# A fused cross-attention and FFN kernel: FFN tiles of 512 tokens in place of 256, raw weights rounded in place

## What is computed

```python
kv = (ctx @ W_src.T + b_src) * mask[:, :, None]        # keys 256, values 256
q  = (layernorm(x) @ W_tgt.T + b_tgt) * mask[:, :, None]
a  = softmax(where(mask == 0, -inf, q_h @ k_h.T / sqrt(32)))   # 8 heads of 32, per sequence
x  = x + concat(layernorm(x), a @ v) @ W_out.T + b_out
n  = layernorm(x)
h  = silu((n @ w1.T) * s1) * ((n @ w2.T) * s2)         # 256 -> 1024, weights in {-1, 0, 1}
h  = gelu((h @ h1.T) * s3)                             # 1024 -> 1024
h  = gelu((h @ h2.T) * s4)                             # 1024 -> 1024
out = x + (h @ w3.T) * s5                              # 1024 -> 256
```

## Time and profile before

| | |
|---|---|
| runs | median 1019.88 us of 3 (1019.52 to 1020.92) |
| profiled execution, first to last instruction | 1017.2 us (no other time of it is given) |
| busy | PE 968.1 us (95%), PEld 919.0, DVE 594.4 (58%), ACT 407.0 (40%), POOL 55.4 |
| chain that ended last, share of the span | PE 89%, DVE 6%, issue 3%, ACT 1%, DMA 1% |
| mean granted TensorE clock | 0.983 |
| HBM | 28.48 MB read, 4.19 MB written, 32 GB/s over the span |

### The profile page before, as it was taken

The page is one execution under the profiler, slowest core; times in us unless marked ns, Lnnn a source line. Parts: engine busy times, 40 slices in busy tenths (PEclk is TensorE's granted clock), DMA queues, the critical chain, the costliest instruction groups (busy, mean ns, idle before and its releaser), DMA issues.

```text
span 1017.2 us, 21299 instructions
## 1 busy us (share of the span) xinstructions
PE 968.1 (95%) x7936; PEld 919.0 (90%) x7936; DVE 594.4 (58%) x1232; ACT 407.0 (40%) x1110; POOL 55.4 (5%) x89
## 2 busy tenths in 40 slices
PE   5468999999999999999999999999999999999998
PEld 4268999999999999999999999999999999999998
DVE  5876464745747465574746657474574646556452
ACT  4735252352525325252432625234262523526231
POOL 1010000001000000100001010000100000010000
PEclk8779999999999999999999999999999999999999
DMA  8621010000001000000100001000000100000000
GB/s 315 220 83 38 9 41 1 21 26 21 26 0 46 0 21 26 21 26 0 41 5 21 26 10 36 0 21 26 21 26 0 46 0 21 26 10 0 0 11 11
DMA packets 18311, 32.99 MB, mean 32 GB/s; under 512 B 4336, under 2 KB 10864, under 8 KB 18288
## 3 DMA queue, kind: packets, MB, share of 16 engines
q1 hardware_dynamic: 18288, 32.68, 9.8%
HBM read 28.48 MB, written 4.19 MB: 32 GB/s over the span
## 4 chain that ended last, share of the span: by engine, by line
PE 89%; DVE 6%; issue 3%; ACT 1%; DMA 1%; SPq 1%; DVEq 0%; POOL 0%; ACTq 0%
PE F L413 57%; PE F L478 6%; PE G L386 6%; PE G L337 5%; PE G L320 5%; PE G L363 3%; PE G L329 3%; DVE pr L740 2%; PE G L374 2%; PE S L349 1%; DVE stage L915 1%; DVE g L794 1%; PE G L310 1%; DVE hAh L811 1%; PE G L396 1%
## 5 line engine op out<-in xcount | busy, mean ns | idle before, releaser
L413 PE MATMUL F<-hBh,H 128*128 128x256 f32 x1024 | 253.4, 289 | 0.7 <-DVE hBl L813 0.7
L413 PE MATMUL F<-hAh,H 128*128 128x256 f32 x1024 | 252.1, 288 | 0.5 <-DVE hAl L813 0.5
L413 PE MATMUL F<-hBl,H 128*128 128x256 f32 x1024 | 245.1, 282 | 0.0
L413 PE MATMUL F<-hAl,H 128*128 128x256 f32 x1024 | 244.9, 281 | 0.0
L574 ACT ACTIVATE g<-F,scols 128x256 f32<-128x256 f32 x256 | 107.4, 471 | 292.7 <-PE F L413 292.5
L413 PEld LDWEIGHTS F<-hAh,H 128*128 128x128 f32 x1024 | 193.0, 188 | 4.2 <-issue 2.8
L413 PEld LDWEIGHTS F<-hBh,H 128*128 128x128 f32 x1024 | 193.5, 189 | 1.7 <-DVE hBl L813 0.9
L413 PEld LDWEIGHTS F<-hAl,H 128*128 128x128 f32 x1024 | 193.7, 189 | 0.4
L413 PEld LDWEIGHTS F<-hBl,H 128*128 128x128 f32 x1024 | 193.3, 189 | 0.7
L413 PE MATMUL F<-x2h,W 128*128 128x256 f32 x512 | 132.6, 298 | 0.4
L811 DVE CAST hAh<-g 128x512 fp32r<-128x512 f32 x128 | 54.7, 427 | 120.6 <-ACT g L574 119.0
(11 more groups left out here) (80 smaller groups left out, 1253.1 us busy)
## 6 DMA issues: line engine op xcount, KB each, us to landing
cT<-ctx_t SPq DMA_DIRECT2D x16, 512.0 KB, 3.3
stage<-h SPq DMA_DIRECT2D x10, 512.0 KB, 5.6
x_in<-x_t SPq DMA_DIRECT2D x16, 256.0 KB, 2.6
out<-sil_y SPq DMA_DIRECT2D x32, 128.0 KB, 1.7
stage<-w SPq DMA_DIRECT2D x6, 512.0 KB, 7.0
mrow<-mask_row SPq DMA_DIRECT2D x16, 128.0 KB, 3.2
g<-h SPq DMA_DIRECT2D x3, 512.0 KB, 6.1
sil_y<-h SPq DMA_DIRECT2D x3, 512.0 KB, 6.2
```

What stands on the lines that cost most here:

```text
L413: ins = mm(bank, W[:, k, cols], part[:, k, :], start=first, stop=last)
```

## The change

**512 tokens.** `WIDE` = 512 and `TILES` = 8. The buffers `x2h`, `x2l`, `hAh` to `hBl`, `g`, `sil`, `x1` and `res` hold 512 tokens, F0 and F1 one block of 512 columns each. Each FFN matmul before W3 has 512 moving columns in place of 256, and there are half as many. W3's matmuls keep their 256 columns (its weights move, the tokens are stationary), and their number stays.

**Slots.** A tile is a list of 44 slots. Slots 0 to 7 are one gate and one up block each, 8 to 39 half a block each of the middle layers, 40 to 43 W3 for four groups of 128 tokens (`j`), of which the last two reuse F0 and F1. The attention works on halves of 256 tokens: half 0 in slots 0 to 21, half 1 in slots 22 to 43, at the same positions (`pos`) in each.

**Weights.** Every piece lands in the memory of its own weight buffer (`W1_raw` is the same bytes as `W1`), DVE looks at its low 16 bits first (a maximum over 1024 16-bit values), and ACT casts it in place. All 22 looks and casts stand in the prologue, which now holds both halves of the first 512 tokens, one look in each even slot and one cast in each odd one.

**Small ones.** `res` is written by ACT (`keep_residual`) and also takes the result; `pT` and `vb` are gone (the transposed probabilities go back into `pr`, `v` is scaled in place); WO is loaded ahead of the first piece; the flag is read once.

```diff
+HALVES = B // NB
+WIDE = 2 * T
+TILES = B * P // WIDE
+NJ = WIDE // P
...
+SLOTS = 44
+HALF = SLOTS // 2
...
-        stage = [sb(f"stage{i}", [P, CH]) for i in range(4)]
+        def with_raw(name, k, m):
+            at_byte = -(-nc.sbuf_base // 32) * 32
+            rounded = sb(name, [P, k, m], F32R)
+            return rounded, nc.alloc_sbuf_tensor_at(name + "_raw", [P, k, m], F32, offset=at_byte)
+        W1, W1_raw = with_raw("W1", KD, HID)
...
-        F = [st.enter_context(nc.psum_tensor(f"F{i}", [P, 2, T], F32)) for i in range(2)]
+        x2h, x2l = sb("x2h", [P, KD, WIDE], F32R), sb("x2l", [P, KD, WIDE], F32R)
+        hAh, hAl = sb("hAh", [P, KH, WIDE], F32R), sb("hAl", [P, KH, WIDE], F32R)
+        hBh, hBl = sb("hBh", [P, KH, WIDE], F32R), sb("hBl", [P, KH, WIDE], F32R)
+        g, sil = sb("g", [P, 2, WIDE]), sb("sil", [P, 2, WIDE])
+        F = [st.enter_context(nc.psum_tensor(f"F{i}", [P, WIDE], F32)) for i in range(2)]
...
-        landing = [s[:] for s in stage] + [g[:].rearrange("p q h t -> p (q h t)"), sil_y[:]]
...
+            def load_chunk(n):
+                src, _, raw, ks = chunks[n]
+                sp.dma_start(raw[:, ks, :], src[:, ks, :]).then_inc(chunk_loaded[n], 16)
...
+            sp.dma_start(WO[:], woT).then_inc(wo_loaded, 16)
+            sp.dma_start(scols[:], s_cols).then_inc(scales_loaded, 16)
+            sp.dma_start(s3_bc[:], s3.broadcast_to([P, D])).then_inc(scales_loaded, 16)
+            for n in range(2 * KD + KH):
+                load_chunk(n)
+            load_tile(1)
+            for n in range(2 * KD + KH, CHUNKS):
+                load_chunk(n)
+            load_tile(2)
...
+            def attention(a, pos):
+                if pos == 0:
+                    transposes_x(a)
+                if pos == 1:
+                    project_k(a)
+                    project_q(a)
...
+                if pos == 8:
+                    project_v(a, 0)
+                    project_v(a, 1)
...
+                if pos == 18:
+                    out_proj(a, 1)
+                if pos == 19:
+                    transpose_x2(a, 0)
+                if pos == 21:
+                    transpose_x2(a, 1)
...
+            def gate_up(f, m, general):
+                pe.wait_ge(x2_ready, at("x2_ready", 2 * f + 1, 2))
+                if m == 0:
+                    pe.wait_ge(scaled, at("scaled", f - 1, 3))
+                else:
+                    pe.wait_ge(sil_ready, at("sil_ready", f, m))
+                cols = slice(m * P, (m + 1) * P)
+                for k in range(KD):
+                    ins = group(F[0][:], W1, W1_raw, k, cols, x2h, x2l, KD - 1, general)
+                ins.then_inc(gate_done, 1)
+                if m == 0:
+                    pe.wait_ge(scaled, at("scaled", f - 1, 4))
+                else:
+                    pe.wait_ge(g_ready, at("g_ready", f, m))
+                for k in range(KD):
+                    ins = group(F[1][:], W2, W2_raw, k, cols, x2h, x2l, KD - 1, general)
+                ins.then_inc(up_done, 1)
...
+                if j >= 2:
+                    pe.wait_ge(scaled, at("scaled", f, j - 1))
...
+            def ffn(f, slot, general):
+                if slot < 8:
+                    gate_up(f, slot, general)
+                elif slot < 40:
+                    half = slot % 2
+                    middle(f, 8 + (slot - 8) // 2, range(4 * half, 4 * half + 4), general)
+                elif slot == 40:
+                    ffn_out(f, 0, range(7), general)
+                    ffn_out(f, 1, range(7), general)
+                elif slot == 41:
+                    ffn_out(f, 0, (7,), general)
+                    ffn_out(f, 1, (7,), general)
                 else:
...
+                    ffn_out(f, slot - 40, range(8), general)
+            def tile(f, s, general):
+                for slot in range(SLOTS):
+                    if s is not None:
+                        attention(2 * s + slot // HALF, slot % HALF)
+                    if f is not None:
+                        ffn(f, slot, general)
...
-            def silu(f, q):
-                act.wait_ge(gate_done, at("gate_done", f, q + 1))
-                for p in (2 * q, 2 * q + 1):
-                    act.wait_ge(g_ready, at("g_ready", f, max(p - 1, 0)))
-                    fn(sil[:, p % 2, :], F[0][:, p % 2, :], ACT.Silu, scale=scols[:, p:p + 1]).then_inc(sil_ready, 1)
+            def silu(f, m):
+                act.wait_ge(gate_done, at("gate_done", f, m + 1))
+                act.wait_ge(g_ready, at("g_ready", f, max(m - 1, 0)))
+                act.wait_ge(y_ready, at("y_ready", f - 1, 4))
+                fn(sil[:, m % 2, :], F[0][:], ACT.Silu, scale=scols[:, m:m + 1]).then_inc(sil_ready, 1)
...
+                if pos == 8:
                     exps(a, 0)
                     exps(a, 1)
+                    scale_v(a)
...
+            def keep_residual(f):
+                act.wait_ge(x1_ready, at("x1_ready", 2 * f + 1, 2))
+                act.wait_ge(stored, at("stored", f - 1, 64))
+                fn(res[:], x1[:], ACT.Copy).then_inc(res_ready, 1)
+            def ffn(f, slot):
+                if slot < 8:
+                    silu(f, slot)
+                    if slot == 2:
+                        keep_residual(f)
+                elif slot < 40 and slot % 2:
+                    gelu(f, 8 + (slot - 8) // 2)
...
+                act.wait_ge(chunk_looked, n + 1)
+                fn(W[:, ks, :], raw[:, ks, :], ACT.Copy).then_inc(chunk_cast, 1)
+            def tile(f, s):
+                for slot in range(SLOTS):
+                    if s is not None:
+                        attention(s, slot // HALF, slot % HALF)
+                    if f is not None:
+                        ffn(f, slot)
+                    elif slot % 2:
+                        cast(slot // 2)
...
+            def attention(s, h, pos):
+                a = 2 * s + h
+                if pos == 0:
+                    mask_bias(a)
+                if pos == 1:
+                    bias_mask_k(a)
+                    bias_mask_q(a)
+                if pos == 2:
+                    mask_scores(a, 0)
+                if pos == 3:
+                    row_max(a, 0)
+                if pos == 4:
+                    mask_scores(a, 1)
+                if pos == 5:
+                    row_max(a, 1)
...
+                if pos == 19:
+                    dve.wait_ge(up_done, at("up_done", s - 1, 8))
+                    x2_lo(a, h, 0)
+                    ln2_apply(a, h, 1)
+                if pos == 21:
+                    x2_lo(a, h, 1)
...
+            def gate_times_up(f, m):
+                dve.wait_ge(up_done, at("up_done", f, m + 1))
+                dve.wait_ge(h_ready, at("h_ready", f, max(m - 1, 0)))
+                dve.wait_ge(sil_ready, at("sil_ready", f, m + 1))
+                V.scalar_tensor_tensor(g[:, m % 2, :], F[1][:], scols[:, KH + m:KH + m + 1],
+                                       sil[:, m % 2, :], ALU.mult, ALU.mult).then_inc(g_ready, 1)
...
+                elif slot == 41:
                     scale_out(f, 0)
                     scale_out(f, 1)
                     add_residual(f, 0)
                     add_residual(f, 1)
...
+                elif slot == 42:
+                    scale_out(f, 2)
+                elif slot == 43:
+                    scale_out(f, 3)
+                    add_residual(f, 2)
+                    add_residual(f, 3)
...
+                low = raw[:, ks, :].bitcast(U16).rearrange("p k (m two) -> p (k m) two", two=2)[:, :, 0]
+                V.tensor_reduce(low_bits[:, n:n + 1], low, AX.X, ALU.max).then_inc(chunk_looked, 1)
...
+            def tile(f, s, last=False):
+                for slot in range(SLOTS):
+                    h, pos = slot // HALF, slot % HALF
+                    if s is not None:
+                        attention(s, h, pos)
+                    if f is not None:
+                        ffn(f, slot)
+                    elif slot % 2 == 0:
+                        look(slot // 2)
+                    if s is not None and not (last and h == 1):
+                        next_norm(2 * s + h + 1, pos)
```

687 lines of the change are left out of this document (233 added, 454 removed).

## The result

The changed kernel takes 1084.3 us (median of 4 runs, 1083.6 to 1086.1) against 1019.7 for the kernel before: ratio 1.064, 95% interval 1.062 to 1.065. It is slower, as forecast, but by 65 us in place of 9, and outside the range that I gave. The profiled execution spans 1083.1 us. I forecast 1026 for that span; the 57 us between the two are the subject of what follows.

A forecast was written before the change was run, and what follows sets the result against it. PE bounds all but the prologue, DVE close behind in the gate phase. Prologue 111, seven tiles 830, first tile's extra 2, last tile 79.2, end 3.7: span 1026, plus 2.7 for the median: 1028.6 us, range 1006 to 1060.

The forecast's parts named there:

- Part 1, wider matmuls: FFN matmuls before W3: one of 512 columns takes 215.7 ns, saving 6.7 us per 512 tokens, 53.5 us in all.
- The excess vanishes when the array has 512 cycles of work per weight block: FFN matmuls: the 11.6 ns over at 256 fp32r columns shrinks as in the fp32 pass, 2.3 over; hence 215.7 ns.
- the pace per column stays: FFN matmuls, within rival 2: a column still costs 0.46 ns, so width gains nothing; +53.5 us, 1082; chance 0.12.
- My other reading: fp32r matmuls of 256 columns: 11.6 of 118.3 ns at the high clock belong to something that doesn't scale with the clock.
- Part 2, the gate phase: Half 0's gate phase: PE stands 4.6 us per 512 tokens for DVE's queue, 18.1 us against 13.5 for PE alone.
- my queue: DVE's list in half 0's gate phase: blocks, masks and maxima end at 17.1 us, giving 18.1 with hand-over and block.
- Rival 3: Gate phase: DVE's backlog is smaller, PE stands 0.5 us in place of 4.6; 29 us less, 1000; chance 0.12.
- The 0.25 us that I put for a `gelu` of half 1: Slot 30 onward: the `gelu` freeing F1 ends after 11.3 us, PE's cover is 11.2; 0.25 us lost.
- Part 3, the end of a tile: Slots 41 and 42: W3's third group waits for DVE's first scaling; PE stands 1.45 us, without attention 0.45.
- Part 4, the prologue: Both halves' attention before the first FFN tile, which starts at 111 us; a look costs 1.2; bounds 101 and 118.
- Rival 4: Prologue: looks fall into waits counted apart, 96 us in place of 111; time 1014; decides at 100; chance 0.13.
- The last tile: Final 512 tile without attention beside it: 79.2 us, including 2.0 for the gate phase's loop; the end another 3.7.

The follow-up runs named there:

- the short maxima: Changed kernel with half 0's two row maxima beside an FFN tile taken over 8 of 128 scores of a head: 1071.2 us.
- The order edit: Changed kernel with DVE doing W3's first two scalings ahead of the x2 remainder and the next half's layernorm statistics ahead of the split: 1065.4 us.
- the kernel before with v moved: Kernel before the change, with v of the first sequence projected ahead of the second sequence's scores: 1009.2 us, ratio 0.989 to before.
- The bunched looks: Changed kernel with scalings, layernorm, masks and maxima reordered (1055.2 us), plus the prologue's looks and casts in bunches where their engine waits: 1046.9 us.

## Why the prediction was right and wrong

| term | forecast | measured |
|---|---|---|
| first FFN tile starts | 111 | 111.13 |
| fp32r matmul, 512 columns | 215.7 ns | 233 ns |
| end of `project_q` to `project_v`, half 0 | 18.1 | 19.1 |
| scaling in slot 42 | 1.45 | 1.2 |
| wait for half 1's layernorm | none | 1.7 |
| steady 512 tile | 118.6 | 125.9 |
| extra of the first tile | 2 | 1.5 |
| last tile alone and the end | 82.9 | 89.1 |
| span | 1026 | 1083.1 |

**Part 1, wider matmuls: the step that failed.** "The excess vanishes when the array has 512 cycles of work per weight block" is wrong. The excess over the array's cycles grows with the columns. In fp32r it is 11.6 ns at 256 columns and 19.7 at 512 (118.3 and 233.0), of which only some 3.6 ns is fixed; in bf16 it is 6.9 and 13.8 (113.6 and 227.1), with nothing fixed. Zero weights and the absence of attention change nothing in it. The nearest row that I took, the fp32 pass, keeps the array busy for 512 cycles with 256 columns. It says nothing on a new column in each cycle. I had named this gap and put 0.12 on "the pace per column stays". That rival gave 1082 and was nearly right in its mechanism: 3.6 ns in 236.6 are won, 1.15 us per 512 tokens where I forecast 6.7. That its number lies so near the measured 1084.3 is in part luck, since it held neither these 9 us won nor the layernorm's wait below, some 12 us lost. The term is 2560 x 17.3 ns = 44 us of the 57.

My other reading, that what doesn't scale with the clock must be fixed per matmul, fell too. At the low clock a column costs its cycle exactly, at both widths (213 and 427 ns). At the high clock each costs more than one.

**Part 2, the gate phase: right in its mechanism, its size in part by luck.** 19.1 us in place of 18.1 from the last `project_q` (498.03) to

```profile
517.17 1.02 PE L277 MATMUL G<-WV,cT 128*128 128x256 f32 x4
```

PE's own work in it is 7 x 1.87 + 1.46 = 14.5, so it stands 4.6 us, as forecast. Two misses cancel in that. With matmuls of 233 ns PE has 1.0 us more work there, and by my queue alone some 3.8 of standing would have been left. But the queue itself was 0.8 longer than worked out, and this is where. DVE's timeline, and GpSimd's one row beside it:

```profile
503.69 0.82 DVE L757 CAST hAh<-g 128x512 fp32r<-128x512 f32 x1
504.54 1.10 DVE L759 TENSOR_TENSOR hAl<-g,hAh 128x512 fp32r<-128x512 f32 x1
...
507.79 0.43 DVE L757 CAST hAh<-g 128x512 fp32r<-128x512 f32 x1
508.25 0.69 DVE L759 TENSOR_TENSOR hAl<-g,hAh 128x512 fp32r<-128x512 f32 x1
```

```profile
503.49 1.60 POOL L846 TENSOR_TENSOR x<-x_in,bo_bc 128x256 f32<-128x256 f32 x2 [14.18 <-ACT res L554]
```

The cast and the subtraction take 0.82 and 1.10 while GpSimd's `add_bias` runs, 0.43 and 0.69 when it doesn't. `keep_residual`, which I had costed at nothing, releases `add_bias` just there. The slow `xn` of 1.53 us above, too, has an `add_bias` beside it (554.10 to 555.55). Over the whole trace all 7 casts and all 7 subtractions of a split that overlap an `add_bias` are slow (0.80 or more, and 1.10), and none of the other 185 of each is. Still this is read from overlaps alone; no run moved `add_bias`. Rival 3 (a smaller backlog) is refuted by the 19.1 us and by the short maxima: 2.01 us out of the list, 1.98 off the tile. My figures for the new forms held: 749 ns for DVE's multiplication of 512 against 742, and 688 for `silu` against 0.69. The 0.25 us that I put for a `gelu` of half 1 shows in no row, and my own 11.3 against 11.2 gave only 0.1.

**Part 3, the end of a tile: right in place, but a term was missing.** The scaling costs 1.2. The sum has no term for the start of half 1, and gives no reason for that; PE waits 1.7 there. I hadn't asked what the list makes the next half's statistics wait for: a split that waits for ACT. The order edit takes out this wait and all but 0.3 of the other, and the tile is 2.87 shorter. Over seven tiles the layernorm's wait is 12 us of the miss. The tile is then 118.6 + 5.5 for the width + 1.7 for this wait, 125.8 for the measured 125.9. That this closes so well hides 0.5 us that the sum had too much (0.25 at the scaling, 0.25 at the `gelu`) and some half a microsecond that no row names.

**Part 4, the prologue: right.** Every milestone fell within a microsecond. A look over 16-bit data takes 1.21 us, as forecast:

```profile
L798 DVE TENSOR_REDUCE low_bits<-H_raw 128x1 f32<-128x1024 uint16 x16 | 19.2, 1209 | 0.0
```

The Trainium skill ("VectorE: DVE Perf Modes", perf-mode tier table) has `tensor_reduce` in its 1x form only, and the trace agrees: 1209 ns for 1024 elements of 16 bits, 1214 for 1024 of fp32 (`row_max`).

Rival 4 (looks fall into waits, a prologue under 100) is refuted by the 111.13, and without looks the start comes 24.3 us earlier, so most of them did not lie in waits.

**The last tile** is off by 6.2 us, of which the width is 320 x 17.3 ns = 5.5.

**Is there a 512-token version that wins?** None that I ran. Without any stall a 512 tile would be 2 x 59.6 less 320 x 3.6 ns, 118.1 us. With the changed kernel's prologue and last tile the span would be 111.1 + 7 x 118.1 + 1.5 + 89.1 = 1028, still above 1017. Against before, the wider tile wins 9 us by its matmuls, and the 25.5 of the balance mostly by having one tile alone of 512 in place of the two of 256 that stood at the ends; it pays 52.7 in the prologue. Only a prologue below some 100 us could turn that, with all stalls gone, and against the kernel before with v moved (span 1008.4) it would have to be some 91. The bunched looks reached 97, but with stalls of 4.4 us a tile.

## What to carry to other kernels

Before a wider matmul is credited with less overhead, ask whether the excess over the array's cycles is per matmul or per column. Two widths of the same type tell; the same width at both clocks does not, and it misled me here. A larger tile also makes the part that must run before the first tile larger, and that part is latency, which no later throughput gives back. And when TensorE waits for one engine's queue, move into that place work that needs TensorE alone. One moved call did this in both kernels, for some 10 us each by their steady tiles.

## What the hardware showed that I had not expected

- At the high clock a column costs 0.443 ns in bf16 with no fixed part (227 ns for 512, 113.6 for 256), and 0.448 in fp32r with some 3.6 ns a matmul on top (233 and 118.3); at the low clock 0.83 in both, its cycle exactly. In fp32 a pass of 256 columns stays at 215.6, 2.3 over its 512 cycles.
- PE waited 1.7 us in the mean, up to 2.1, at each return to the loop's start when one turn had 2078 instructions of PE, and not with 1437.
- The records of waits understate them: 0.64 in the record was worth 0.70 when taken away, and 2.7 was worth 2.87.
- DVE's cast and subtraction took 0.4 us more each, and a pair of `tensor_scalar` 0.8, beside GpSimd's two additions of 256 elements.
